# Cross-attention with a gated residual on one core: output scaling, squares and loads in another order

## The chip, the cores and the metric

The kernel runs on one core of a Trainium2 chip. The metric is the device time of one execution in microseconds (us). Engines are named as in the profile: PE is TensorE (PEld its weight loads), DVE is VectorE, ACT is ScalarE, POOL is GpSimd, SP is SyncE, whose queue issues every DMA of this kernel.

## The reference, cut to what matters

```python
def rmsnorm(v, w):
    return v * rsqrt(mean(v * v, -1) + 1e-6) * w
mem = einsum('bme,de->bmd', memory, W_mem)                # memory: 4 x 2048 x 512
scores = einsum('bnd,bmd->bnm', x, mem) / sqrt(1024)      # x: 4 x 1024 x 1024
attn = softmax(scores, -1)
context = einsum('bnm,bmd->bnd', attn, mem)
gate = sigmoid(concat([x, context], -1) @ W_gate.T + b_gate)
out = rmsnorm(x + gate * context, norm_w)                 # 4 x 1024 x 1024, fp32
```

## The kernel before

All products are fp32 in three passes: an operand is split into a high part (a cast by ACT) and a low part (a subtraction by DVE, line 305), and TensorE computes high x high, high x low and low x high into one PSUM bank. The 4096 rows of x are 32 units of 128 rows, or 16 pairs.

**Stages.** First (to about 500 us) projected queries and the x part of the gate (`zx`) are computed and stored in DRAM. Then comes the attention over the 32 units, 8 to a batch. Last comes the gate part over the 16 pairs, whose products use a seven-product scheme (Winograd's form of Strassen) with `gate_product` and `context_product`; each is 6 matmuls.

**Attention.** In step i TensorE computes the scores of unit i+1 (48 matmuls into banks 0 to 3, `scores`) and then the attention product of unit i (48 matmuls, four groups, one for each memory block). DVE takes the maxima (line 1190), ACT the exponentials (line 782). The probabilities have to be transposed over all partitions: SP stores them in DRAM and reads them back in another layout (`exchange`: stores at line 496, read back at line 502), then DVE transposes 32 x 32 blocks into PSUM (line 1219), and ACT and DVE split them. The queries of unit i+2 are loaded (line 457), cast by ACT (line 774) and their low part made by DVE (`q_split`) behind unit i+1's exponentials. TensorE waits for them (`uq_ready`) ahead of the next scores. Once per batch the memory is loaded in two layouts: `load_mt` (line 246) for the scores, `load_mn` (line 447) for the attention product, four blocks of 1 MB each. In the step that uses a new batch's first attention product (`mn_of`), some of the blocks are split ahead of the loop over groups and the others inside it; for the first unit that number is `MN_FIRST`. SP is one queue in program order: block loads, exchange, query loads and stores of results stand behind each other.

**Gate part.** TensorE's order in a pair p is gate 1, context 7 of pair p-1, gate 2, gate 3, then context 1, gate 4, context 2, gate 5, context 3, gate 6, context 4, gate 7, context 5, context 6 (`pair_c` at the end of the program). `pair_c` of DVE evacuates the gate products (`gate_part`, line 1272), multiplies gate and context (`gated`, line 1286), adds x (`residual_unit`, line 1299), transposes and splits the next pair's operands (`transpose_am`, `sums_of_am`, `split_at`) and scales a unit of an older pair (`scale`, line 1292) for its store. ACT's `pair_act` copies context products (`copy_c`, lines 860 and 869), takes sigmoids (`gate`), casts operands (`split_at`, line 796) and squares each finished unit with a sum over its row (`square`, line 875). POOL turns that sum into the root's inverse (`inverse_root`, lines 659 and 662). The result tiles `c_u` are two, one for each parity of the pair: before pair p writes `c_u[par]`, the store of pair p-2 must have landed (`out_stored`). Gate product 1 of a pair waits for all six gate evacuations of the pair before (`gz_ev`), context product 7 for context part 5.

The last pair ends with its four half units by hand: residuals (line 1495), a whole-unit square by ACT (line 935), two half squares by DVE (line 1500), a sum of the two (line 1517), POOL's two roots, `scale` of the first unit and two half scalings (line 1522).

## Time and profile before

| what | value |
|---|---|
| times of 3 runs | 1571.56, 1575.01, 1575.78 us (median 1575.01) |
| profiled execution | 1575.41 us, its span 1573.6 us |
| PE busy | 1536.4 us (98%), 6720 matmuls |
| DVE busy | 1078.2 us (69%) |
| ACT busy | 541.9 us (34%) |
| POOL busy | 36.4 us (2%) |
| DMA | 262.60 MB, mean 167 GB/s |
| granted TensorE clock, mean | 0.995 |

A time in the rows is counted from the first instruction of the span. Matmuls are pipelined and their ends are modelled, so a busy PE is not PE at its peak; the distance of starts tells its pace. A name such as `region_f` is a large SBUF region that holds many tiles; which one it is follows from the line.

### The profile page before, as it was taken

What the parts mean: (1) busy time and instruction counts of PE and PEld (TensorE: products, weight loads), DVE (VectorE), ACT (ScalarE), POOL (GpSimd) and SP (SyncE); (2) the same over time, 40 slices, a digit from 0 to 9 for tenths busy, and PEclk for the clock granted to TensorE, in tenths of its full rate; (3) what the DMA queues carried; (4) which work ended last, traced back from release to release, by engine and by line L of the source; (5) the groups of instructions that cost most, each with busy time, mean ns of one, the idle gap of its engine ahead of it and who ended that gap; (6) DMA issues with size and microseconds to landing.
All of it is one profiled execution on the core that took longest, in us unless ns stands there. A gap on an engine that the chain in (4) does not pass through costs nothing.

```text
span 1573.6 us, 21461 instructions
## 1 busy us (share of the span) xinstructions
PE 1536.4 (98%) x6720; PEld 1263.1 (80%) x6720; DVE 1078.2 (69%) x1505; ACT 541.9 (34%) x915; POOL 36.4 (2%) x70
## 2 busy tenths in 40 slices
PE   7999999999999989999999999999999999999997
PEld 5888888888888768888888878788788888788885
DVE  5654758777778754567437764577555888888887
ACT  4233342222222332244222532244222544444443
POOL 0000000000000000000000000000000001111111
PEclk9999999999999999999999999999999999999998
DMA  9998436333332866757584666747758645555553
GB/s 198 233 236 186 116 96 176 107 113 107 107 107 94 189 165 172 180 140 191 157 203 132 164 161 176 177 136 190 184 153 267 227 159 190 186 192 191 188 194 135
DMA packets 213398, 262.60 MB, mean 167 GB/s; under 512 B 19312, under 2 KB 136048, under 8 KB 213104
## 3 DMA queue, kind: packets, MB, share of 16 engines
q1 hardware_dynamic: 213360, 262.20, 59.5%
q14 instruction: 28, 0.23, 0.1%
q8 instruction: 10, 0.16, 0.0%
HBM read 170.39 MB, written 89.65 MB: 165 GB/s over the span
## 4 chain that ended last, share of the span: by engine, by line
PE 33%; DMA 13%; DVE 6%; issue 5%; SPq 3%; ACT 2%; DVEq 0%; ACTq 0%; POOL 0%; POOLq 0%
PE bank L1530 23%; PE bank L1662 10%; DMA prob_scratch<-prob 5%; DMA out<-region_f 3%; DMA region_f<-in_ctx 2%; SPq L246 2%; DMA region_f<-prob_scratch 2%; DMA am_out<-q_scratch 1%; DVE region_l L305 1%; DVE region_f L1286 1%; DVE max_part L1190 1%; DVE region_f L1292 1%; SPq L447 1%; ACT prob L782 1%; DVE region_n L305 0%
## 5 line engine op out<-in xcount | busy, mean ns | idle before, releaser
L1530 PE MATMUL bank<-region_t,region_l 128*128 128x512 f32 x1536 | 356.1, 391 | 8.4 <-DVE region_l L305 6.2
L1530 PE MATMUL bank<-region_n,region_l 128*128 128x512 f32 x1536 | 355.7, 391 | 4.1 <-DVE region_n L305 2.1
L1530 PEld LDWEIGHTS bank<-region_t,region_l 128*128 128x128 f32 x1536 | 288.9, 188 | 71.7 <-issue 11.7
L1530 PEld LDWEIGHTS bank<-region_n,region_l 128*128 128x128 f32 x1536 | 289.2, 188 | 65.7 <-issue 4.1
L1530 PE MATMUL bank<-region_t,region_n 128*128 128x512 f32 x960 | 220.4, 392 | 11.2 <-DVE region_t L305 11.2
L1530 PEld LDWEIGHTS bank<-region_t,region_n 128*128 128x128 f32 x960 | 181.7, 189 | 49.4 <-DVE region_t L305 11.6
L810 ACT CAST region_l<-bank 128x512 fp32r<-128x512 f32 x128 | 75.0, 586 | 347.2 <-DVE bank L1219 347.0
L1219 DVE STREAM_TRANSPOSE bank<-region_f 128x512 f32<-128x512 f32 x128 | 88.8, 716 | 121.7 <-DMA region_f<-prob_scratch 119.5
L305 DVE TENSOR_TENSOR region_t<-region_f,region_t 128x1024 fp32r<-128x1024 f32 (+2 forms) x77 | 110.6, 1468 | 76.4 <-ACT region_t L686 57.4
L1571 PE MATMUL bank<-region_t,region_l 128*128 128x512 f32 x576 | 135.8, 389 | 0.0
L1571 PEld LDWEIGHTS bank<-region_t,region_l 128*128 128x128 f32 x576 | 108.1, 188 | 22.4
L1662 PE MATMUL bank<-region_t,region_l 128*128 128x512 f32 x480 | 121.9, 392 | 1.8 <-DVE prob L1272 0.9
L1662 PE MATMUL bank<-region_n,region_l 128*128 128x512 f32 x480 | 120.6, 389 | 0.0
L782 ACT ACTIVATE prob<-bank,neg_max 128x512 f32<-128x512 f32 x128 | 86.2, 686 | 76.1 <-DVE neg_max L1196 72.9
L1662 PEld LDWEIGHTS bank<-region_t,region_l 128*128 128x128 f32 x480 | 89.2, 188 | 24.4 <-issue 6.4
L1662 PEld LDWEIGHTS bank<-region_n,region_l 128*128 128x128 f32 x480 | 90.0, 188 | 19.3 <-DVE region_f L1286 0.4
L737 ACT CAST region_l<-region_f 128x512 fp32r<-128x512 f32 x80 | 49.5, 623 | 158.7 <-PE bank L1571 146.5
L305 DVE TENSOR_TENSOR region_l<-region_f,region_l 128x512 fp32r<-128x512 f32 (+2 forms) x120 | 81.8, 686 | 17.8 <-ACT region_l L796 17.1
L305 DVE TENSOR_TENSOR region_l<-bank,region_l 128x512 fp32r<-128x512 f32 x128 | 86.6, 676 | 9.9 <-ACT region_l L810 9.8
L1571 PE MATMUL bank<-region_n,region_l 128*128 128x512 f32 x384 | 92.2, 389 | 0.0
L1190 DVE TENSOR_REDUCE max_part<-bank 128x1 f32<-128x512 f32 x128 | 84.4, 660 | 10.2 <-PE bank L1530 10.2
L305 DVE TENSOR_TENSOR region_n<-region_f,region_n 128x512 fp32r<-128x512 f32 (+3 forms) x70 | 78.5, 1141 | 14.6 <-ACT region_n L682 7.7
(81 smaller groups left out, 1421.9 us busy)
## 6 DMA issues: line engine op xcount, KB each, us to landing
region_f<-in_ctx SPq DMA_DIRECT2D x128, 256.0 KB, 5.4
prob_scratch<-prob SPq DMA_DIRECT2D x128, 256.0 KB, 2.7
region_f<-prob_scratch SPq DMA_DIRECT2D x128, 256.0 KB, 4.4
region_f<-in_x SPq DMA_DIRECT2D x64, 256.0 KB, 6.1
region_f<-in_x SPq DMA_DIRECT2D x128, 128.0 KB, 2.7
region_f<-in_x SPq DMA_DIRECT2D x16, 1024.0 KB, 8.1
out<-region_f SPq DMA_DIRECT2D x31, 512.0 KB, 7.1
q_scratch<-prob SPq DMA_DIRECT2D x8, 1024.0 KB, 6.3
```

Source lines behind the costliest of these rows:

```text
L246: eng.dma_start(v[SQ * q:SQ * (q + 1), :, lo:hi], src[:, chunk * q + lo:chunk * q + hi].rearrange("(b i) f -> i b f", i=SQ)).then_inc(sign ...
L305: return nc.vector.tensor_tensor(dst, src, hi.bitcast(F32), ALU.subtract)
L447: sp.dma_start(v[SQ * q:SQ * (q + 1)], mem[b, r:r + P, :].rearrange("(s i) c -> i s c", i=SQ)).then_inc(mn_loaded[j], 16)
L737: nc.scalar.copy(z_x[i][:, HI], quarter(z_f[i])).then_inc(z_hi, 1)
L782: nc.scalar.activation(prob[:, BANK * j:BANK * (j + 1)], bank[j][:], ACT.Exp, bias=neg_max[:], scale=SCALE, accum_out=sum_part[:, j:j + 1] ...
L810: nc.scalar.copy(b_pt[:, HI, TPB * g:TPB * (g + 1), :].rearrange("p k n -> p (k n)"), ps_t[g % 2][:]).then_inc(pt_hi, 1)
L1190: nc.vector.reduce_max(max_part[:, j:j + 1], bank[j][:], AX_X).then_inc(max_done, 1)
L1219: nc.vector.transpose(ps_t[g % 2][:].rearrange("p (k b i) -> p k b i", k=TPB, i=SQ), v[:, TPB * g:TPB * (g + 1)]).then_inc(pt_t, 1)
L1286: nc.vector.tensor_tensor(quad(c_u[par], u, h), src, quad(c_gate[par], u, h), ALU.mult).then_inc(gc_ev, 1)
L1530: mm = nc.tensor.matmul(dst, lhs(a), rhs(b), start=first and n == 0, stop=last and n == len(PASSES) - 1)
L1571: mm = nc.tensor.matmul(ps[:], z_x[i][:, a, t, :], z_w[i][:, b, t, :], start=opens and t == 0 and n == 0, stop=closes and t == HT - 1 and ...
L1662: mm = nc.tensor.matmul(ps[:], x[:, a, P * t:P * (t + 1)], w[n][:, b, t, :], start=opens and t == 0 and m == 0, stop=closes and t == CH - ...
```

## The change

In the attention the first unit's third memory block is loaded ahead of the first exchange and split ahead of the loop (`MN_FIRST` 3). In the four steps with `mn_of` the queries are split before the exponentials. In the two steps with `mt_ahead` DVE's four memory transposes stand behind the row sums and the query split.

In the gate part, ACT squares the pair before's units at the start of a pair, and context product 2's copy comes before product 3's. DVE scales the units of pair p-1 in pair p; before it scaled those of pair p-2. SP issues its loads and stores in a matching order. In the last pair the squares are taken by half units, three by ACT and one by DVE, POOL adds the halves, and DVE's first two residuals and the gating between them move ahead of other work.

```diff
@@ -289,7 +289,7 @@
 MTS = MB * HPJ
-MN_FIRST = 2
+MN_FIRST = 3
 MN_EARLY = 2
@@ -324,7 +324,7 @@
 U11, U22_OPEN, U12_OPEN, U22, U12, U21 = range(1, 7)
-COPY_B, COPY_12, COPY_22 = range(1, 4)
+COPY_B, COPY_22, COPY_12 = range(1, 4)
 GATE = {(0, 0): 1, (1, 1): 2, (0, 1): 3, (1, 0): 4}
@@ -514,9 +514,9 @@
 load_mn(0, 0)
-exchange(0, first=True)
 sp.wait_ge(mt_ready, HPJ * 3)
 load_mn(0, 2)
+exchange(0, first=True)
 sp.wait_ge(mt_ready, MTS)
@@ -616,29 +616,26 @@
-def pair_out(p, par, ahead=True, stored=True, am_ahead=True):
+def pair_out(p, par, ahead=True, am_ahead=True):
+    sp.wait_ge(fused_done, p * 2)
+    load_xres(p)
     if ahead:
         sp.wait_ge(gc_ev, p * NGEV)
         load_zx(p + 1, 1 - par)
-    sp.wait_ge(fused_done, p * 2)
-    load_xres(p)
-    if stored:
-        for u in range(2):
-            store_out(p - 2, par, u)
     if am_ahead:
         sp.wait_ge(ca_t, p * 2 + 4)
         load_am(p + 2)
+    for u in range(2):
+        store_out(p - 1, 1 - par, u)
 sp.wait_ge(ca_t, 4)
 load_am(2)
-pair_out(1, 1, stored=False)
+pair_out(1, 1)
 with sp.Fori(1, NPAIR // 2 - 1) as i:
...
 pair_out(NPAIR - 1, 1, ahead=False, am_ahead=False)
-for u in range(2):
-    store_out(NPAIR - 2, 0, u)
 store_out(NPAIR - 1, 1, 0)
@@ -654,8 +651,8 @@
-def inverse_root(p, u, last=0):
-    pool.wait_ge(sq_done, p * 2 + (u + 1 + last))
+def inverse_root(p, u):
+    pool.wait_ge(sq_done, p * 2 + (u + 1))
     nc.gpsimd.tensor_tensor(mean_sq[:, u:u + 1], sq_mean[:, u:u + 1], norm_eps[:], ALU.add
@@ -670,8 +667,20 @@
 pair_pool(NPAIR - 2, 0)
-inverse_root(NPAIR - 1, 0)
-inverse_root(NPAIR - 1, 1, last=2)
+def last_root(u, first, second):
+    a, b = (sum_part[:, 2 * u + h:2 * u + h + 1] for h in (u, 1 - u))
+    pool.wait_ge(sq_done, NUNIT - 2 + first)
+    nc.gpsimd.tensor_tensor(mean_sq[:, u:u + 1], a, norm_eps[:], ALU.add).then_inc(var_done, 1)
+    pool.wait_ge(sq_done, NUNIT - 2 + second)
+    pool.wait_ge(var_done, NUNIT - 2 + 2 * u + 1)
+    nc.gpsimd.tensor_tensor(mean_sq[:, u:u + 1], mean_sq[:, u:u + 1], b, ALU.add).then_inc(var_done, 1)
+    pool.wait_ge(var_done, NUNIT - 2 + 2 * u + 2)
+    nc.gpsimd.tensor_tensor(rstd[:, u:u + 1], mean_sq[:, u:u + 1], m_half[:], ALU.pow
+                            ).then_inc(rstd_done, 1)
+last_root(0, 1, 3)
+last_root(1, 2, 4)
@@ -815,9 +824,11 @@
 if softmax:
+    if mn_of is not None:
+        q_split(i + 2)
     act.wait_ge(sum_done, i + 1)
     exps(i + 1)
-    if unit_after_next:
+    if mn_of is None and unit_after_next:
         q_split(i + 2)
@@ -878,32 +889,28 @@
 seed_z(p)
+square(p - 1, 1 - par, 0, wait=i is not None)
+square(p - 1, 1 - par, 1)
 copy_c(p, 1, cb[:], ca)
-gate(p, par, 0, 0, Z11)
 if following:
     act.wait_ge(gc_prod, p * NPROD)
     act.wait_ge(ca_t, p * 2 + 4)
     split_at(1 - par, at_12, atf_12)
+gate(p, par, 0, 0, Z11)
+if i is not None:
+    act.wait_ge(out_stored[par][1], i * 16)
+copy_c(p, 2, quad(c_u[par], 1, 1), cf)
+if following:
+    act.wait_ge(ca_sum, p * 4 + 8)
+    split_at(1 - par, at_s, atf_s)
 gate(p, par, 1, 1, Z22)
...
 if following:
-    act.wait_ge(ca_sum, p * 4 + 8)
-    split_at(1 - par, at_s, atf_s)
-if i is not None:
-    act.wait_ge(out_stored[par][1], i * 16)
-copy_c(p, 2, quad(c_u[par], 1, 1), cf)
-if following:
-    gate(p, par, 0, 1, Z12)
     split_at(1 - par, at_22, atf_22)
-square(p - 1, 1 - par, 0, wait=i is not None)
-if following:
-    gate(p, par, 1, 0, Z21)
-square(p - 1, 1 - par, 1)
-if not following:
-    gate(p, par, 0, 1, Z12)
-    gate(p, par, 1, 0, Z21)
+gate(p, par, 0, 1, Z12)
+gate(p, par, 1, 0, Z21)
...
@@ -930,10 +937,12 @@
 pair_act(NPAIR - 1, 1, NPAIR // 2 - 1, following=False)
-act.wait_ge(fused_done, 2 * (NPAIR - 1) + 3)
-act.wait_ge(sq_done, NUNIT - 2)
-nc.scalar.activation(c_square, unit_tile(c_u[1], 0), ACT.Square, scale=float(D) ** -0.5,
-                     accum_out=sq_mean[:, 0:1]).then_inc(sq_done, 1)
+for n, (u, h) in enumerate(((0, 0), (1, 1), (0, 1))):
+    act.wait_ge(fused_done, 2 * (NPAIR - 1) + n + 1)
+    act.wait_ge(sq_done, NUNIT - 2 + n)
+    nc.scalar.activation(c_square[:, 0:BANK], quad(c_u[1], u, h), ACT.Square, scale=float(D) ** -0.5,
+                         accum_out=sum_part[:, 2 * u + h:2 * u + h + 1]).then_inc(sq_done, 1)
@@ -1303,37 +1312,49 @@
     gate_part(p, par, 2, zf, 1, 1)
-    if i is not None:
-        scale(p - 2, par, 0)
     gate_part(p, par, 3, za, 0, 1)
-    if i is not None:
-        scale(p - 2, par, 1)
+    if following:
+        transpose_am(p + 1, c_ain_units)
     gate_part(p, par, 4, zb, 0, 0)
     if following:
-        transpose_am(p + 1, c_ain_units)
+        sums_of_am(p + 1)
     gate_part(p, par, 5, za, 1, 1, Z22_OPEN)
     if following:
-        sums_of_am(p + 1)
         split_at(p + 1, 1, 1 - par, at_12, atf_12)
+    scale(p - 1, 1 - par, 0)
     gate_part(p, par, 6, zf, 0, 1, Z12_OPEN)
     if following:
         split_at(p + 1, 2, 1 - par, at_s, atf_s)
+    else:
+        scale(p - 1, 1 - par, 1)
     if i is not None:
         dve.wait_ge(out_stored[par][0], i * 16)
+    gated(p, par, 0, 0, cb[:], product=4)
     if not following:
-        scale(p - 1, 1 - par, 0)
-    gated(p, par, 0, 0, cb[:], product=4)
+        residual(0, 0, U11)
     gate_part(p, par, 7, za, 1, 0)
     if following:
         split_at(p + 1, 3, 1 - par, at_22, atf_22)
+        scale(p - 1, 1 - par, 1)
     context_part(p, par, 5, COPY_22, ca, 1, 1)
-    if not following:
-        scale(p - 1, 1 - par, 1)
     if following:
         context_part(p, par, 6, COPY_12, cf, 0, 1)
-        gated(p, par, 1, 1, quad(c_u[par], 1, 1), opened=U22_OPEN)
-        gated(p, par, 0, 1, quad(c_u[par], 0, 1), opened=U12_OPEN)
+    gated(p, par, 1, 1, quad(c_u[par], 1, 1), opened=U22_OPEN)
+    if not following:
+        residual(1, 1, U22 - 1)
+        context_part(p, par, 6, COPY_12, cf, 0, 1)
+    gated(p, par, 0, 1, quad(c_u[par], 0, 1), opened=U12_OPEN if following else U12_OPEN + 1)
+    if following:
         residual_unit(p, par, 0)
+LP = NPAIR - 1
+def residual(u, h, count):
+    v = quad(c_u[1], u, h)
+    dve.wait_ge(xres_loaded, NPAIR * 16)
+    dve.wait_ge(gc_ev, LP * NGEV + count)
+    nc.vector.tensor_tensor(v, v, quad(c_xres, u, h), ALU.add).then_inc(fused_done, 1)
@@ -1356,9 +1377,8 @@
     unit_max(i + 1)
-if mt_ahead is not None:
-    for h in mt_ahead[1]:
-        mt_transpose(mt_ahead[0], h)
+if mn_of is not None:
+    q_split(i + 2)
 if mt_of is not None:
@@ -1370,8 +1390,11 @@
     unit_sum(i + 1)
-    if unit_after_next:
+    if mn_of is None and unit_after_next:
         q_split(i + 2)
+if mt_ahead is not None:
+    for h in mt_ahead[1]:
+        mt_transpose(mt_ahead[0], h)
 if mt_of is not None:
@@ -1484,37 +1507,16 @@
         pair_c(i * 2 + par, par, i)
-LP = NPAIR - 1
 pair_c(LP - 1, 0, NPAIR // 2 - 1)
 pair_c(LP, 1, NPAIR // 2 - 1, following=False)
-def residual(u, h, count):
-    v = quad(c_u[1], u, h)
-    dve.wait_ge(gc_ev, LP * NGEV + count)
-    nc.vector.tensor_tensor(v, v, quad(c_xres, u, h), ALU.add).then_inc(fused_done, 1)
-def last_square(h, count):
-    v = quad(c_u[1], 1, h)
-    dve.wait_ge(fused_done, 2 * LP + count)
-    nc.vector.tensor_tensor_reduce(out=quad(c_gate[0], 1, h), in0=v, in1=v, scale=1.0 / D, scalar=0.0,
-                                   op0=ALU.mult, op1=ALU.add, accum_out=sum_part[:, h:h + 1]
-                                   ).then_inc(sq_done, 1)
-dve.wait_ge(xres_loaded, 16 * NPAIR)
-residual(0, 0, U11)
-context_part(LP, 1, 6, COPY_12, cf, 0, 1)
-gated(LP, 1, 1, 1, quad(c_u[1], 1, 1), opened=U22_OPEN)
-gated(LP, 1, 0, 1, quad(c_u[1], 0, 1), opened=U12_OPEN)
-residual(1, 1, U22)
 residual(0, 1, U12)
 gated(LP, 1, 1, 0, ca[:], product=7)
 residual(1, 0, U21)
-dve.wait_ge(sq_done, LP * 2 + 1)
-last_square(1, 2)
-last_square(0, 4)
+v = quad(c_u[1], 1, 0)
+dve.wait_ge(fused_done, 2 * LP + 4)
 dve.wait_ge(sq_done, LP * 2 + 3)
-nc.vector.reduce_sum(sq_mean[:, 1:2], sum_part[:, 0:DH], AX_X).then_inc(sq_done, 1)
+nc.vector.tensor_tensor_reduce(out=quad(c_gate[0], 1, 0), in0=v, in1=v, scale=1.0 / D, scalar=0.0,
+                               op0=ALU.mult, op1=ALU.add, accum_out=sum_part[:, 2:3]).then_inc(sq_done, 1)
 scale(LP, 1, 0)
```

## Rows read from the trace of the kernel before

**Rows 1.** Windows: busy us (count) of each engine, granted clock, DMA share, GB/s.

```profile
660.00:750.00 90.00, 90.00 (x399) 74.55 (x398) 65.15 (x94) 37.38 (x64) 0.00 (x0) 1.00 0.61 164
...
550.60:554.00 3.40, 3.40 (x9) 2.64 (x8) 1.51 (x3) 3.40 (x4) 0.00 (x0) 0.51 0.75 219
...
1308.00:1560.00 252.00, 250.44 (x1093) 203.91 (x1092) 218.12 (x320) 111.59 (x195) 31.27 (x56) 1.00 0.51 183
...
1561.70:1573.60 11.90, 0.11 (x1) 0.00 (x0) 8.52 (x16) 1.15 (x2) 3.26 (x4) 0.61 0.34 132
```

**Rows 2.** Timeline of PE, pieces with idle time before: start, us, engine, line, idle.

```profile
562.99 5.74 PE L1530 MATMUL bank<-region_n,region_l 128*128 128x512 f32 x24 [1.07 <-DVE region_l L305]
...
570.84 7.52 PE L1530 MATMUL bank<-region_n,region_l 128*128 128x512 f32 x24 [2.11 <-DVE region_n L305]
...
579.69 11.19 PE L1530 MATMUL bank<-region_t,region_l 128*128 128x512 f32 x48 [1.33 <-DVE region_l L305]
...
755.10 11.19 PE L1530 MATMUL bank<-region_t,region_l 128*128 128x512 f32 x48 [0.52 <-DVE region_l L305]
...
930.91 11.19 PE L1530 MATMUL bank<-region_t,region_l 128*128 128x512 f32 x48 [1.00 <-DVE region_l L305]
...
998.59 11.17 PE L1530 MATMUL bank<-region_t,region_l 128*128 128x512 f32 x48 [2.03 <-DVE region_l L305]
...
1108.81 11.15 PE L1530 MATMUL bank<-region_t,region_l 128*128 128x512 f32 x48 [1.13 <-DVE region_l L305]
```

**Rows 3.** Waits in the gate part: us in total, times, longest.

```profile
ACT region_f L869 <- DMA out<-region_f: 28.4, 11, 3.1
```

**Rows 4.** Timeline of all engines, one pair of the gate part.

```profile
1510.29 2.16 SPq L592 DMA_DIRECT2D out<-region_f  x2
...
1518.40 1.05 ACT L796 CAST region_t<-region_f 128x1024 fp32r<-128x1024 f32 x1
...
1522.04 1.65 PE L1662 MATMUL bank<-region_t,region_l 128*128 128x512 f32 x6
...
1522.36 0.55 POOL L662 TENSOR_TENSOR rstd<-mean_sq,minus_half 128x1 f32<-128x1 f32 x1
```

**Rows 5.** Timeline of all engines, behind the last product.

```profile
1564.77 0.69 DVE L1286 TENSOR_TENSOR region_f<-bank,region_f 128x512 f32<-128x512 f32 x1
...
1567.83 1.28 DVE L1292 SCALAR_TENSOR_TENSOR region_f<-region_f,rstd 128x1024 f32<-128x1024 f32 x1 [0.24 <-POOL rstd L662]
...
1568.03 1.49 POOL L662 TENSOR_TENSOR rstd<-mean_sq,minus_half 128x1 f32<-128x1 f32 x1
...
1569.56 1.42 DVE L1522 SCALAR_TENSOR_TENSOR region_f<-region_f,rstd 128x512 f32<-128x512 f32 x2 [0.44 <-POOL rstd L662]
```

**Rows 6.** Timeline of SP, DVE and ACT, the first unit of the attention.

```profile
542.70 1.76 SPq L447 DMA_DIRECT2D region_f<-in_ctx  x4
...
549.01 1.67 SPq L496 DMA_DIRECT2D prob_scratch<-prob  x3
...
551.58 0.34 SPq L502 DMA_DIRECT2D region_f<-prob_scratch  x1
...
560.45 1.32 DVE L1219 STREAM_TRANSPOSE bank<-region_f 128x512 f32<-128x512 f32 x2 [3.15 <-DMA region_f<-prob_scratch]
...
565.30 1.91 ACT L766 CAST region_n<-region_f 128x2048 fp32r<-128x2048 f32 x1 [2.92 <-DMA region_f<-in_ctx]
...
569.90 1.90 ACT L766 CAST region_n<-region_f 128x2048 fp32r<-128x2048 f32 x1 [2.20 <-DMA region_f<-in_ctx]
```

**Rows 7.** Timeline of SP and DVE at later steps.

```profile
638.41 1.55 SPq L496 DMA_DIRECT2D prob_scratch<-prob  x3
...
644.98 0.35 SPq L502 DMA_DIRECT2D region_f<-prob_scratch  x1
...
812.88 0.72 SPq L457 DMA_DIRECT2D am_out<-q_scratch  x1
...
1116.33 1.32 DVE L1219 STREAM_TRANSPOSE bank<-region_f 128x512 f32<-128x512 f32 x2 [6.62 <-DMA region_f<-prob_scratch]
```

More of the change, by code:

```diff
@@ L917, in _ @@
             gate(0, 0, 1, 1, Z22)
+            copy_c(0, 2, quad(c_u[0], 1, 1), cf)
             copy_c(0, 3, quad(c_u[0], 0, 1), ca)
-            copy_c(0, 2, quad(c_u[0], 1, 1), cf)
             act.wait_ge(ca_t, 4)
```

## The prediction

> **What bounds it.** I read the engines' busy shares first: TensorE is at 98%, so only time in which it waits or runs slow can be won. Its pace comes from a window without a wait: 90 us hold 397 to 399 matmuls, 0.2267 us each, so 48 of them, one unit's scores or one unit's attention product, take 10.9 us [rows 1]. All 6720 need 1523 us of a span of 1573.6; about 50 us are left, and about 10 of those are the start, before the first matmul. I then read TensorE's pieces that have idle time before them [rows 2] and looked up what each waited for.
>
> The first unit of the attention loses most: 1.1 us before its first product at 562.99, 2.1 us before 570.84 (the third memory block's low part), 1.3 us before 579.69 (the queries of the next unit) [rows 2]. After idle times of 2 us the granted clock falls to half: 9 matmuls in 3.4 us instead of 15 [rows 1], so 6 x 0.2267 = 1.4 us are lost each time. At each change of batch the queries come late: 0.5, 1.0 and 1.1 us (755.10, 930.91, 1108.81), and once more by 2.0 us at 998.59 [rows 2]. In the gate part a window of 252 us holds 1093 matmuls, worth 247.8 us: 4.2 us are lost in small pieces, though VectorE is busy for 218 and ScalarE for 112 of it, 16.5 and 8.4 us per pair of 84 matmuls (19.04 us) [rows 1]. Last, 11.9 us lie behind TensorE's last product at 1561.7 [rows 1].
>
> **Gate part.** One pair shows the stall. The output store of the pair two back is issued at 1510.29, while two loads of 1 MB are under way; ScalarE may overwrite that buffer only when it has landed, 7.6 us later, and only then casts the next operand, at 1518.40; VectorE waits for the cast, and its gate part 7 behind that lets TensorE go on at 1522.04 [rows 4]. Such waits of ScalarE sum to 28.4 us in 11 pairs [rows 3]. The change scales a pair one pair earlier. I lay VectorE's new list over TensorE's order, counted from gate product 1: the fourteen products of 1.36 us end at 1.4 (gate 1), 2.7 (context 7 of the pair before), 4.1, 5.4 (gate 2, 3), 6.8 (context 1), 8.2 (gate 4), 9.5, 10.9, 12.2, 13.6 (context 2, gate 5, context 3, gate 6), 15.0, 16.3, 17.7, 19.0 (context 4, gate 7, context 5, 6); what reads one begins 0.2 us later; half a unit takes VectorE 0.6 to 0.7 us, a whole one 1.2 to 1.3 [rows 5]. That gives: gate part 5 at 11.1 to 11.7, a split to 12.3, the scaling of unit 0 to 13.6, gate part 6 to 14.4, the wide split to 15.6, the gating to 16.2, gate part 7 at 16.5 to 17.2, a short split to 17.6, the scaling of unit 1 to 18.9, context part 5 to 19.5. The stores follow, and the buffer is wanted 9.7 us into the next pair (behind context 2): 9.7 + 19.0 - 18.9 = 9.8 us for a landing that took 7.6. So that wait goes. What is late next? VectorE's work is the same, 16.5 of 19.0 us. Gate part 7 is done at 17.2 and needed at 19.0. Context part 5, now behind a split and a scaling, is done at 19.5; product 7, which waits for it, comes at 20.4. The two squares that ScalarE now does first (1.25 us each, estimated from 1.28 for a scaling of the same tile) end near 6.6 us, and the copy behind them has its product at 6.8. The cast that held VectorE comes behind the sums, which end near 10.6, takes 1.05 us [rows 4], ends near 11.6 and is needed at 14.4. Each has 0.9 us or more to spare, so I count the whole 4.2 us. Half of it is the lower end. The reordered queue of SyncE loads xres first and the zx tile next; both had over 10 us, nothing waits for them. New waits of SyncE for the scaling hold up only the next pair's load of x, which starts 5.4 us into the pair, 5.6 us later.
>
> **Tail.** Before, gated part (1,0) ran at 1564.77, though its product ended at 1561.7 [rows 1, 5]; VectorE was still at a scaling, two residuals and two gatings. Three of these move ahead of the last product, so it can run near 1562.8: 2.0 us. One of VectorE's two last squares (0.6) goes to ScalarE, and its sum (0.15 us) goes: the last square ends 2.6 us earlier. But GpSimd has two additions per unit now and a power behind each pair. Its power took 0.55 us beside a quiet VectorE and 1.49 us (from 1568.03) beside the scaling of 1.28 us at 1567.83 [rows 4, 5]. In the new order the second unit's second addition comes behind the start of that scaling: so it ends after it, the power after that (0.25 + 0.55 + two handovers of 0.1), about 1.0 us behind the scaling's end; before it was 0.45. The first root is ready near 1565.5 (2.3 us earlier), scaling till 1566.8, the second root 1567.8, where the last scaling began at 1569.56: **1.8 us** won. If additions were not held up, 2.4.
>
> The Trainium skill (SBUF — State Buffer, section "SBUF: two separate sides") says that a VectorE operation with both inputs in SBUF locks a port pair that GpSimd's reads need, so that the loser fully blocks. By that rule the tail wins 1.8 us; without it, 2.4. The 1.49 against 0.55 us agrees with the rule.
>
> **Attention, first unit.** The third memory block's load moves ahead of the exchange of the first unit. This is the part that costs. Two blocks landed 4.6 us apart (565.30 and 569.90) [rows 6], so two of them, the first issued at 542.70, fill the queues to about 542.7 + 9.2 = 551.9. The probability stores are issued at 549.01 and the first read back at 551.58, 2.57 us later [rows 6]. Behind the second block they land at about 551.9 + 2.57 = 554.5: 2.9 us late, and everything of the exchange with them. Bounds: 0 (they pass the block) and 4.0, from a later exchange behind twelve loads, where the same step took 6.57 us (638.41 to 644.98) [rows 7]. I take 2.9. The transposition at 560.45 and the product at 562.99 go to 563.3 and 565.9. TensorE then idles 4.0 us and runs slow for a slice behind it (1.4 us). In exchange the third block's casts are done before (three casts of 1.9 us [rows 6] and three low parts little longer fit between the exponentials, near 551, and 563.3), the fourth lands near 568, its casts end near 573.5, and TensorE needs it after 36 matmuls and the slow slice, at 575.5: both other stalls and the other slow slice go. The queries, cast ahead of the exponentials, are there by 570. Scores of the next unit begin at 565.9 + 10.9 + 1.4 = 578.2 instead of 579.69: **1.5 us**. Without the delay, 574.0: 5.7 us. With 4.0 us of delay, 0.4 us.
>
> **Attention, queries at the batch changes.** They stop being late there (0.5, 1.0 and 1.1 us). But what TensorE wins against the exchange it may lose again. At the first two the next wait is the query load, issued behind twelve block loads at 812.88 [rows 7] and its like before 998.59; those come behind the exchange in SyncE's queue, and the exchange doesn't move. I count 0 there. At the third no such wait follows; the next transposition starts at 1116.33, and by the 2.54 us between 560.45 and 562.99 the product can start at 1118.9, where it started at 1108.81 + 11.0 = 1119.8 [rows 2, 6, 7]: **0.9 us**. The transpositions moved behind the queries (four of 1.2 us) end 2 us before the next exchange lands: 0.
>
> **Sum.** 4.2 + 1.8 + 1.5 + 0.9 = 8.4 us off the profiled execution's 1575.41, which is 0.4 above the median 1575.01: 1567.0.
>
> **Rivals.** A: the stores pass the block load. Against: 6.57 us behind loads [rows 7]. For: that queue was longer, with small pieces. It gives 4.2 us more: **1562.8**, chance 0.2. The Trainium skill (DMA: Bandwidth & Descriptors, section "Queues, rings and completion order") says that an engine takes a ring's descriptors in order; by it A can't be. B: the gate part keeps half its stalls because VectorE, 87% busy, is late after its two scalings: 4.2 / 2 less, **1569.1**, chance 0.15; for it speaks that 0.9 us of room is small. C: the batch-change wins stay (0.5 + 1.0 more): **1565.5**, chance 0.15. D, slower: the stores, now issued at the pair's end, run into the loads of the next pair and take long. The point is 9.8 us, and as the cast has 2.8 us more room, 12.6 in all. At 13.5 us each pair stalls 0.9 us, 14 x 0.9 = 12.6, which takes the place of the 4.2 lost now: 1567.0 + 12.6 = **1579.6**, chance 0.03. Against: 7.6 us with both loads in flight [rows 4]. E: the change does nothing in the attention, 2.4 us less won: 1569.4, 0.07. My forecast has 0.4.
>
> **Numbers.** A measurement can tell about 0.3%, 4.7 us, so the mark is 1570.3. The range reaches from A, with a bit for C beside it, to B and E with the runs' spread: 1562 to 1571. Faster 0.87, within 0.3% 0.1, slower 0.03.
>
> **What would show it.** The wait of ScalarE's context copies for the output stores gone [rows 3], and no idle TensorE piece in the gate part from the third pair. One idle piece of about 4 us before the first unit's product, then half clock, and none before the third block. Idle of 1 us or so where the first two batches' gains are given back, and a later q wait grown by as much. The last scaling begins 8 us earlier than 1569.56. Wrong if the first exchange isn't late, if SyncE's stores take over 10 us, or if context part 5 holds product 7.

## The result and the profile after

The changed kernel takes **1569.90 us** (median of 20 runs, 1567.14 to 1571.97). The kernel before takes 1572.92 us in the same series (20 runs, 1569.89 to 1575.88), so two of the three runs known ahead of the prediction (1575.01 and 1575.78; median of the three 1575.01) lay at the slow end of its own spread. The ratio is 0.998, interval 0.9973 to 0.9987: 3.0 us faster. A second series gave 0.9979 (0.997 to 0.9987). That is real, but less than the 0.3% set as the mark, and 2.9 us short of the forecast 1567.0.

The profiled execution took 1568.30 us, span 1566.5 (before: 1575.41 and 1573.6). To see where 7.1 us of span went I take the start of the n-th matmul on TensorE, which is the same work in every kernel here, and add up by stretch. "First unit" is the 96 matmuls from the scores of unit 1 (n = 2352) to the scores of unit 2 (n = 2448); "gate part" runs from the first full pair (n = 5478) to the last product (n = 6719), "tail" from that product's start to the end of the span.

| stretch, us | before | after | after, again |
|---|---|---|---|
| start to n = 2352 | 549.13 | 549.28 | 548.59 |
| first unit | 30.56 | 31.62 | 29.69 |
| rest of attention to n = 5478 | 695.60 | 693.59 | 696.61 |
| gate part | 286.13 | 281.43 | 281.43 |
| tail | 12.17 | 10.55 | 10.56 |

**Gate part.** Windows of the kernel after (us, then busy time and count of PE, PEld, DVE, ACT, POOL; granted clock; DMA share; GB/s), for a stretch of the gate part, the tail, and the half-clock stretch of the first unit:

```profile
1300.00:1552.00 252.00, 252.00 (x1113) 208.67 (x1112) 224.03 (x324) 117.70 (x196) 25.30 (x52) 1.00 0.49 186
1556.20:1566.50 10.30, 0.11 (x1) 0.00 (x0) 6.32 (x10) 1.12 (x4) 3.39 (x5) 0.67 0.26 102
...
566.40:573.20 6.80, 6.20 (x15) 4.85 (x16) 6.46 (x10) 3.50 (x5) 0.00 (x0) 0.50 0.23 48
```

252 us now hold 1113 matmuls where they held 1093 [rows 1]: TensorE is at its pace of 0.2267 us throughout. ScalarE's waits in the gate part say why. In the kernel after:

```profile
ACT bank L871 <- PE bank L1664: 38.1, 14, 2.7
ACT region_f L876 <- DVE region_f L1281: 36.0, 30, 2.6
ACT prob L876 <- DVE prob L1281: 30.3, 28, 2.1
ACT region_n L886 <- DVE region_f L1308: 29.2, 29, 1.3
```

Every wait is for something that is computed; the row that waited for the output stores [rows 3] has no successor. In one pair the stores are issued behind the loads, and the second waits in SyncE's queue for its scaling (timeline of the kernel after):

```profile
1503.00 0.41 SPq L612 DMA_DIRECT2D region_f<-in_x  x1
...
1503.66 0.41 SPq L586 DMA_DIRECT2D prob<-zx_scratch  x1
...
1505.57 0.40 SPq L582 DMA_DIRECT2D region_f<-am_scratch  x1
...
1511.36 5.59 SPq L592 DMA_DIRECT2D out<-region_f  x2
```

By then the loads of x and zx have landed. The page gives the median landing of all 31 stores, in the kernel after and in the kernel before:

```profile
out<-region_f SPq DMA_DIRECT2D x31, 512.0 KB, 2.6
...
out<-region_f SPq DMA_DIRECT2D x31, 512.0 KB, 7.1
```

**First unit.** TensorE's timeline of the kernel after:

```profile
549.28 12.77 PE L1532 MATMUL bank<-region_t,region_l 128*128 128x512 f32 x48 [2.07 <-ACT prob L791]
567.00 14.06 PE L1532 MATMUL bank<-region_n,region_l 128*128 128x512 f32 x48 [4.95 <-DVE region_l L305]
580.90 11.04 PE L1532 MATMUL bank<-region_t,region_l 128*128 128x512 f32 x48
...
767.07 3.23 PE L1532 MATMUL bank<-region_n,region_l 128*128 128x512 f32 x13 [0.62 <-DVE region_l L305]
...
822.88 7.33 PE L1532 MATMUL bank<-region_t,region_l 128*128 128x512 f32 x31 [1.13 <-DVE region_l L305]
```

One idle piece of 5.0 us, then all 48 products in one piece, and no wait for the queries at 580.90: the three waits of before [rows 2] are one. But the clock was at half (1.2 GHz) for 6.8 us from the end of that idle piece on, not for 3.4. The last two rows are the first batch change: TensorE starts its scores without a wait (755.41) and waits at the product behind them, and again at the next query load.

SyncE's timeline of the kernel after shows the price of the early load, 5.86 us from the stores to the first read back instead of 2.57 [rows 6]:

```profile
542.85 3.71 SPq L447 DMA_DIRECT2D region_f<-in_ctx  x8
549.16 1.67 SPq L496 DMA_DIRECT2D prob_scratch<-prob  x3
555.02 0.34 SPq L502 DMA_DIRECT2D region_f<-prob_scratch  x1
```

**Tail.** All engines, timeline of the kernel after, answering to [rows 5]:

```profile
1559.49 1.01 POOL L679 TENSOR_TENSOR rstd<-mean_sq,minus_half 128x1 f32<-128x1 f32 x1
...
1560.47 0.18 POOL L674 TENSOR_TENSOR mean_sq<-sum_part,norm_eps 128x1 f32<-128x1 f32 x1
1560.53 1.28 DVE L1301 SCALAR_TENSOR_TENSOR region_f<-region_f,rstd 128x1024 f32<-128x1024 f32 x1 [0.43 <-POOL rstd L679]
1560.80 1.06 POOL L677 TENSOR_TENSOR mean_sq<-mean_sq,sum_part 128x1 f32<-128x1 f32 x1
1561.84 0.33 SPq L592 DMA_DIRECT2D out<-region_f  x1
1561.94 0.55 POOL L679 TENSOR_TENSOR rstd<-mean_sq,minus_half 128x1 f32<-128x1 f32 x1
1562.52 1.42 DVE L1524 SCALAR_TENSOR_TENSOR region_f<-region_f,rstd 128x512 f32<-128x512 f32 x2 [0.71 <-POOL rstd L679]
```

GpSimd's second addition for unit 1 starts beside VectorE's scaling and ends with it, 1.06 us; the same kind of addition takes 0.18 us a moment earlier. The root is ready 0.7 us behind the scaling.

### The profile page after: what moved, and what is told of

Its sections match the earlier page's. It is cut to its first block, busy times and chain, and to the rows that moved or that the text cites. A ratio compares the mean times of both kernels' runs of the same rounds, so it can differ in the third digit from the quotient of the medians.

```text
span 1566.5 us, 21464 instructions
## 1 busy us (share of the span) xinstructions
PE 1532.7 (98%) x6720; PEld 1264.5 (81%) x6720; DVE 1080.2 (69%) x1502; ACT 549.2 (35%) x919; POOL 33.3 (2%) x72
## 4 chain that ended last, share of the span: by engine, by line
PE 77%; DMA 11%; SPq 4%; DVE 4%; issue 3%; ACT 1%; POOL 0%; ACTq 0%; DVEq 0%; POOLq 0%
PE bank L1532 39%; PE bank L1573 19%; PE bank L1664 19%; DMA prob_scratch<-prob 5%; SPq L246 2%; DMA region_f<-prob_scratch 2%; DMA region_f<-in_ctx 2%; DMA am_out<-q_scratch 1%; DVE region_l L305 1%; DVE max_part L1199 1%; DMA region_f<-in_L_xattn_W_gate 1%; SPq L447 1%; DVE bank L1228 0%; DVE region_n L305 0%; SPq L337 0%
## 5 line engine op out<-in xcount | busy, mean ns | idle before, releaser
L1532 PEld LDWEIGHTS bank<-region_n,region_l 128*128 128x128 f32 x1536 | 290.0, 189 | 70.0 <-DVE region_l L305 5.4
L1532 PEld LDWEIGHTS bank<-region_t,region_n 128*128 128x128 f32 x960 | 181.1, 189 | 50.2 <-DVE region_t L305 12.5
L1664 PEld LDWEIGHTS bank<-region_n,region_l 128*128 128x128 f32 x480 | 90.0, 188 | 19.1 <-DVE region_f L1295 0.4
L1199 DVE TENSOR_REDUCE max_part<-bank 128x1 f32<-128x512 f32 x128 | 84.5, 661 | 12.3 <-PE bank L1532 12.3
L1573 PEld LDWEIGHTS bank<-region_n,region_l 128*128 128x128 f32 x384 | 72.1, 188 | 15.0
```

What stands on the lines that cost most here:

```text
L1199: nc.vector.reduce_max(max_part[:, j:j + 1], bank[j][:], AX_X).then_inc(max_done, 1)
L1532: mm = nc.tensor.matmul(dst, lhs(a), rhs(b), start=first and n == 0, stop=last and n == len(PASSES) - 1)
L1573: mm = nc.tensor.matmul(ps[:], z_x[i][:, a, t, :], z_w[i][:, b, t, :], start=opens and t == 0 and n == 0, stop=closes and t == HT - 1 and ...
L1664: mm = nc.tensor.matmul(ps[:], x[:, a, P * t:P * (t + 1)], w[n][:, b, t, :], start=opens and t == 0 and m == 0, stop=closes and t == CH - ...
```

## The experiments

Twelve kernels ran, each with one profile. The first four shared 35 runs of the kernel before (median 1571.68), the next four 20 (1572.89), the last four 27 (1571.86); ratios are to those.

**1. Load back, the rest changed.**

```
-        MN_FIRST = 3
+        MN_FIRST = 2
...
             load_mn(0, 0)
+            exchange(0, first=True)
             sp.wait_ge(mt_ready, HPJ * 3)
             load_mn(0, 2)
-            exchange(0, first=True)
```

> The changed kernel with its early load taken back: the third block is again loaded behind the first exchange and split inside the loop; the query order, the gate part and the tail stay changed. Theory 1 (the early load delays the first exchange by 4 us and costs more than it gives): the changed kernel lost 1.2 us up to the scores of the third unit against before; without the load the queries ahead of the exponentials should give 1.5 us there instead, so this kernel is 2.5 to 3 us faster than the changed one, about 6 us under the kernel before (ratio 0.996). Theory 2 (the load is a gain or nothing, and the small total comes from elsewhere: the gate part's gain is smaller in most executions than in the profiled one): this kernel is as fast as the changed one or slower, ratio 0.998 or more.

Measured 1569.36 us (12 runs), ratio 0.9984 (0.9974 to 0.9993): the same as the changed kernel, so theory 1 (2.5 to 3 us faster than that) is out. Stores to read back is 2.58 us again, and two stalls are back in other places: 2.8 us inside the first product and 0.7 us ahead of the second unit's. First unit 30.54 us.

**2. The load alone.** The kernel before, with the same five lines of experiment 1 the other way round.

> The kernel before with the early load alone (third block ahead of the first exchange, three blocks split ahead of the loop). Theory 1: one idle piece of 5 us before the first unit's product, two slices at half clock, and in all 1 to 1.5 us slower than before. Theory 2: both later stalls of the first unit go at no price, 4 us faster.

1571.36 us (12 runs), ratio 0.9995 (0.9985 to 1.0004); stores to read back 5.70 us, first unit 30.71. It is neither slower by 1 us nor faster by 4, as the two theories had it. With experiment 1: the early load is worth nothing either way. What it takes away and what it costs are equal within the noise.

**3. Gate part and tail alone.** The new orders of both; load, queries and transpositions as before (in step_act and step_dve):

```
-                    if mn_of is not None:
-                        q_split(i + 2)
                     act.wait_ge(sum_done, i + 1)
                     exps(i + 1)
-                    if mn_of is None and unit_after_next:
+                    if unit_after_next:
                         q_split(i + 2)
...
```

> The kernel before with the gate part's new order and the tail by halves alone (no early load, queries and transposes as before). Both theories put the gain here; by the two profiles the gate part gives 4.7 us and the tail 1.6: 6.3 us under before, ratio 0.996. Theory 2 wants it at 3 us. The difference to the run without the early load is what the query order gives by itself: 1.5 us at the first unit and some tenths at the third batch change by theory 1.

1569.00 us (11 runs), ratio 0.9985 (0.9977 to 0.9994): 2.7 us, as theory 2 had it, and not the 6.3 us of the two profiles. The whole gain of the change is here.

**4. The load sooner.** As changed, but the third block is loaded ahead of SyncE's wait for the zx stores, so that nothing stands behind it but one more block:

```
+            sp.wait_ge(mt_ready, HPJ * 3)
+            load_mn(0, 2)
             for i in range(3):
                 sp.wait_ge(zx_stored[i], 16 * NPAIR)
             load_mn(0, 0)
-            sp.wait_ge(mt_ready, HPJ * 3)
-            load_mn(0, 2)
             exchange(0, first=True)
```

> The changed kernel with the third block's load issued ahead of SyncE's wait for the last zx stores, so about 3 us sooner and ahead of the first block's load in the queue. Theory 1: the queue is empty sooner, the first exchange is 2 us instead of 4 us late, the idle piece before the first unit's product is 3.3 instead of 5.3 us, one slice at half clock instead of two: 2 to 3.4 us faster than the changed kernel. A rival (the delay doesn't come from the queue but from splits of three blocks on ScalarE and VectorE, or from reading back into the same memory): the idle piece stays 5 us and the time that of the changed kernel.

1566.48 us (12 runs), ratio 0.9964 (0.9955 to 0.9974). Stores to read back: 4.65 us. The idle piece ahead of the product was expected at 3.3 us with 3.4 us of half clock behind it; this profile has 6.0 us and 6.8 us, no better than with the load in the changed kernel's place (4.4 to 6.5 us in five profiles). The runs are faster all the same, by 2.9 us against experiment 1 in the same series.

**5. The scaling held.**

```
-            scale(LP, 1, 0)
             dve.wait_ge(rstd_done, NUNIT)
+            scale(LP, 1, 0)
```

> The changed kernel, with VectorE's scaling of the last pair's unit 0 held until GpSimd has the root of unit 1 too. Theory 1 (GpSimd is blocked while VectorE runs an operation with two SBUF inputs): GpSimd's second addition for unit 1, which took 1.06 us beside that scaling, takes 0.2 to 0.3 us again, its power 0.55 us; the root of unit 1 is there about 0.8 us sooner, and the three last scalings run one behind the other: last product to end of span 11.0 us instead of 10.56 (+0.5). Rival (that addition takes about 1 us by itself, for instance because it follows right on another): it still takes 1.06 us, the root comes as late as now, the tail is 11.8 us (+1.3).

GpSimd's timeline of this kernel:

```profile
1563.35 0.18 POOL L674 TENSOR_TENSOR mean_sq<-sum_part,norm_eps 128x1 f32<-128x1 f32 x1
1563.68 0.19 POOL L677 TENSOR_TENSOR mean_sq<-mean_sq,sum_part 128x1 f32<-128x1 f32 x1
1563.95 0.55 POOL L679 TENSOR_TENSOR rstd<-mean_sq,minus_half 128x1 f32<-128x1 f32 x1
```

The addition takes 0.19 us, and the root ends 5.70 us behind the last product's start instead of 6.57, 0.87 us sooner. That settles it for theory 1: GpSimd's operation was blocked by the scaling, it was not slow by itself.

All 14 profiles together show which operations of VectorE block it. Of GpSimd's additions, 263 began while VectorE ran an operation with two inputs in SBUF (residuals, gatings with a copied product, low parts, squares, scalings); every one of them ended 0.04 to 0.05 us behind the end of that operation, and took up to 1.16 us. Another 158 began beside a transpose or beside an operation that reads one input from PSUM; they took 0.19 us, as beside a quiet VectorE. The Trainium skill (SBUF — State Buffer, section "SBUF: two separate sides") has the rule: a VectorE operation with two SBUF inputs and a GpSimd operation that reads SBUF use one port pair in turns, each for its whole instruction. This run and these counts agree with it. The tail, though, is 11.49 us, not 11.0: the scalings end 0.32 us later, and the last stores are now issued 0.7 us behind unit 0's whole store instead of 1.5 and land in 2.6 us instead of 2.0. Its time, 1568.34 us (7 runs, 0.997, 0.9959 to 0.9981), can't show half a microsecond.

**6. Stores ahead of the loads.** The kernel before with one edit in pair_out; scaling, squares and ScalarE's order stay:

```
+                if stored:
+                    for u in range(2):
+                        store_out(p - 2, par, u)
                 if ahead:
                     sp.wait_ge(gc_ev, p * NGEV)
                     load_zx(p + 1, 1 - par)
                 sp.wait_ge(fused_done, p * 2)
                 load_xres(p)
-                if stored:
-                    for u in range(2):
-                        store_out(p - 2, par, u)
```

> The kernel before, whose only edit is in SyncE's queue of the gate part: the two output stores of a pair are issued ahead of the two 1 MB loads of zx and x instead of behind them; the scaling stays where it was, two pairs late. Theory 1 (what stalled the gate part was only the landing of those stores behind loads): stores land in 2.6 to 3.5 us instead of 7, ScalarE's waits for them (28.4 us in 11 pairs before) fall under 5 us, the gate part from gate product 1 to the last product takes 281.4 to 282 us instead of 283.5 to 286.1, the tail stays 12.2 us, and the time is 2 us under the kernel before. Rival A (stores share the engines with whatever is in flight, wherever they stand in the queue): landing stays near 7 us and the gate part at 283.5 or more. Rival B (the loads, now behind the scaling's wait, come late): a new wait for zx or x, gate part over 284 us.

1570.10 us (11 runs), ratio 0.9982 (0.9973 to 0.9991). SyncE's timeline of this kernel, the same pair as [rows 4]:

```profile
1505.51 2.16 SPq L592 DMA_DIRECT2D out<-region_f  x2
1507.92 0.41 SPq L586 DMA_DIRECT2D prob<-zx_scratch  x1
1508.51 0.51 SPq L612 DMA_DIRECT2D region_f<-in_x  x1
```

The pair runs 4.5 us earlier here (what was won till then), so the stores are issued at the same point of it, within 0.3 us; only the loads stand behind them now. From the page, the stores' landing:

```profile
out<-region_f SPq DMA_DIRECT2D x31, 512.0 KB, 2.7
```

No wait of ScalarE for them is left, the gate part takes 281.43 us to the hundredth as in the changed kernel, and the tail is 12.08. Theory 1 holds without remainder: not the lateness of the scaling but the two loads ahead of the stores made the stall. The whole reordering of the gate part is matched by moving three lines of a queue.

**7. Sooner, attention otherwise old.** Experiment 4 with the queries and transpositions put back as in experiment 3.

> As e4_load_sooner (third memory block loaded ahead of the wait for the zx stores), but with the queries behind the exponentials and the transpositions behind the row maxima again, as in the kernel before. It tells whether the early load needs the queries ahead. Theory 1 (what e4 gained over the changed kernel, 3.4 us, is the load's place alone; queries ahead are given back): 1566 to 1567.5 us, the same as e4. Rival (with the load in its place the queries are what is late next, 1.2 us at the third unit and 0.5 to 1.0 at each change of batch): 1568 us or more.

1566.67 us (5 runs), ratio 0.9959 (0.9946 to 0.9972), as experiment 4. The queries ahead add nothing.

**8. Squares whole.** The changed kernel with the last pair's squares of before:

```
-            for n, (u, h) in enumerate(((0, 0), (1, 1), (0, 1))):
-                act.wait_ge(fused_done, 2 * (NPAIR - 1) + n + 1)
...
+            act.wait_ge(fused_done, 2 * (NPAIR - 1) + 3)
+            act.wait_ge(sq_done, NUNIT - 2)
+            nc.scalar.activation(c_square, unit_tile(c_u[1], 0), ACT.Square, scale=float(D) ** -0.5,
...
+            last_square(1, 2)
+            last_square(0, 4)
```

> The changed kernel, with the squares of the last pair as in the kernel before: ScalarE squares unit 0 whole, VectorE both halves of unit 1 behind it and adds them, GpSimd has one addition per unit. The order of the gatings and residuals stays the new one. Theory 1 (GpSimd blocked beside two-input operations of VectorE): the second root comes 0.75 us later at its start, but with one addition less to be blocked; the last scalings start 0.3 us later, tail 10.9 us instead of 10.56; so of the tail's 1.6 us the halves are 0.3 and the order 1.3. Rival (halves are worth what they take off VectorE, 0.6 + 0.15 us): tail 11.3 us or more.

Tail 10.71 us, 0.16 more than with halves: 0.3 was expected, the rival's 0.75 is out. So of the tail's 1.6 us the new order gives 1.5 and "the tail by halves" almost nothing, because VectorE's saved time is spent waiting for a root that is blocked beside the scaling, as these rows of its timeline show:

```profile
1559.67 1.28 DVE L1289 SCALAR_TENSOR_TENSOR region_f<-region_f,rstd 128x1024 f32<-128x1024 f32 x1
1559.84 1.16 POOL L656 TENSOR_TENSOR mean_sq<-sq_mean,norm_eps 128x1 f32<-128x1 f32 x1 [0.48 <-DVE sq_mean L1515]
```

Its time is 1567.54 us (7 runs, 0.9969, 0.9958 to 0.998).

**9 to 12. One more series,** with the changed kernel itself, the sooner load alone on the kernel before, and experiments 3 and 7 again.

> The changed kernel itself once more, so that it stands in one series with the three kernels beside it (the kernel before moved by 1.2 us between two series). Theory 1 (its own gain is 2.5 to 3 us, and the early load behind the zx stores is worth nothing): 2 to 4 us under the kernel before of this series, the same as e11_gate_tail_again within 1.5 us. Rival (the first unit costs it 1 us or more against the old order, as in its one profile, +1.1): e11_gate_tail_again is 1 us or more faster than this.

> The kernel before, and of the change only the third memory block's load, put ahead of the wait for the zx stores. Theory 1 (the place of the load was worth 3 us in e4_load_sooner and is independent of the gate part): 2.5 to 3.5 us under the kernel before, with no TensorE idle time from the queries or the third block at 570 to 580. Rival (what e4 showed was mostly its series and the gate part): within 1 us of the kernel before, as e2_load_alone was; index of the first scores behind the first product (2448) not more than 1 us sooner than before.

> e3_gate_tail_alone again in one series with the others (kernel before with the new order of the gate part and the tail, attention as before). Theory 1: 2.5 to 4 us under the kernel before: the gate part at 281.4 us and the tail at 10.56 us, as in every kernel with these orders. Against e12_best_again it stands for the early load's worth in its best place: by theory 1 it is 2.5 us slower than that, by the rival (that gain was chance) within 1 us.

> e7_sooner_rest_old again, in one series with the changed kernel: gate part and tail new, third memory block loaded ahead of the wait for the zx stores, queries and transpositions as before. Theory 1: 1565.5 to 1567.5 us, 5.5 to 6.5 us under the kernel before and 2 us or more under the changed kernel. Rival (run to run spread made it look better in its series): within 1 us of e11_gate_tail_again and of the changed kernel.

| kernel | median us (runs) | ratio, interval |
|---|---|---|
| changed | 1568.71 (11) | 0.9979, 0.997 to 0.9987 |
| sooner alone | 1570.05 (11) | 0.9988, 0.9979 to 0.9997 |
| gate and tail | 1568.92 (8) | 0.9974, 0.9963 to 0.9985 |
| gate, tail, sooner | 1565.97 (7) | 0.9964, 0.9952 to 0.9977 |

Gate and tail alone equals the whole change again. Sooner alone wins 1.8 us, less than the 2.5 expected, and with gate and tail 5.9 us. That version beats the kernel before in both its series (0.9959 and 0.9964). Against the changed kernel it is 2.7 us faster in the one series that has both, by 7 runs against 11; experiments 5 and 8, the changed kernel but for its tail, were 1.7 and 0.9 us slower than it in the other, the second within the noise. TensorE's timeline of "sooner alone", with idle time of 2.5 us where the changed kernel had 5.0 (the shortest of its kind: the other three profiles with the load there have 3.9, 4.0 and 6.0):

```profile
549.37 12.77 PE L1530 MATMUL bank<-region_t,region_l 128*128 128x512 f32 x48 [2.07 <-ACT prob L782]
564.64 12.57 PE L1530 MATMUL bank<-region_n,region_l 128*128 128x512 f32 x48 [2.50 <-DVE region_l L305]
577.05 8.32 PE L1530 MATMUL bank<-region_t,region_l 128*128 128x512 f32 x36
```

**The first unit over all 14 profiles** (mean and range of each group, us). To product: from n = 2352 to the first product.

| load of the third block | profiles | stores to read back | to product | its 48 products | both |
|---|---|---|---|---|---|
| behind the exchange | 5 | 2.6 | 14.3 | 16.4 | 30.7 (30.2 to 31.2) |
| ahead of it, behind zx stores | 5 | 5.8 | 17.6 | 13.2 | 30.8 (29.7 to 31.6) |
| ahead of the zx stores' wait | 4 | 4.5 | 16.1 | 13.0 | 29.1 (27.7 to 30.6) |

The profiles give the sooner load 1.7 us in this stretch; the timed runs give it 1.8 us by itself and about 3 us with the gate part and the tail. Where the rest of it lies isn't shown.

## Why the prediction was right or wrong

The time lay in the range and on the side said. That is partly luck: the sum was 8.4 us and the gain is 3.0, but the sum was taken off the profiled execution's 1575.41, 2.5 us above the median that 20 runs gave; 8.4 - 3.0 - 2.5 = 2.9 us is the error. The time also lies next to rivals with chances of 0.15 (B, 1569.1) and 0.07 (E, nothing from the attention, 1569.4). E's mechanism is what the runs show in the attention; B's is not what they show in the gate part. Term by term:

**Gate part, 4.2 us.** Mechanism right, and shown twice: by the change itself, and by experiment 6 with the landing alone. The list of VectorE's work held: all 11 profiles in which the stores no longer stand behind the loads have 281.42 to 281.47 us, the pace of TensorE, so rival B (half the stalls stay) and D (stores slow in the next pair's loads; they landed in 2.6) are out. Against the profile of before it won even 4.7. The step that failed is "I count the whole 4.2 us", read as a property of the kernel: the term was too large by 1.1 us. It was one execution's: three profiles with the old gate part lost 4.7, 2.1 and 2.4 us against 281.43, with landings of 6.9 to 7.1 us. The stall hangs on when each landing ends, and the one profile at hand was the worst of three. Their mean, 3.1 us, agrees with what experiment 6 won (2.8). "Half of it is the lower end" was nearer to the truth than the value taken.

**Tail, 1.8 us.** Measured 1.6, in every profile (12.08 to 12.24 before, 10.55 to 10.57 after). The blocked addition came as worked out, and experiment 5 shows it to be the cause. The last scaling began 7.0 us earlier than 1569.56, 8 were said. Two parts were off against each other: the first root came 1.8 us sooner behind the last product's start, not 2.3, and the second was ready 0.7 us behind the scaling's end, not 1.0. VectorE's square and sum that go were put at 0.6 and 0.15 us of the way; experiment 8 finds 0.16 for all that the halves do.

**Attention, first unit, 1.5 us.** The sign of every step was right: the exchange came late by 3.3 us (2.9 said, from the times when two blocks land; rival A, stores pass the loads, would have shown 2.57 us to the read back; it is this measurement that rules it out), and all later waits fell together into one. What failed is the second half: "Scores of the next unit begin at 565.9 + 10.9 + 1.4". The 48 products took 13.2 us on the mean, not 12.3, since behind the one long idle time the clock was at half for 6.8 us in 6 of 9 profiles with the load early in either place, against never more than 3.4 us at a time with the load old. The 48 products took 12.5 us on the mean in the three profiles with 3.4 us of it and 13.4 in the six with 6.8. The slow slice itself was priced low, too: 1.4 us by a count of nine matmuls, where the two pieces of 24 matmuls in [rows 2] differ by 7.52 - 5.74 = 1.8 us. With 0.4 us for the exchange, 0.9 for the products, and 0.3 because the 48 products take 16.4 us on the mean of the old profiles and 16.7 in the one of before, the 1.5 us are gone: measured 0.1 slower.

**Attention, queries, 0.9 us at the third change.** Wrong. The expected win and its counterpart can be laid side by side as the distance from the last matmul ahead of the scores to the scores, plus the distance from there to the next product. Third change: 1.52 + 10.99 = 12.51 us before, 0.23 + 12.00 = 12.23 after; over eight profiles with the queries behind 12.5 on the mean, over six with them ahead 12.6. The step was "the next transposition starts at 1116.33": it started 11.7 to 12.0 us behind the start of the exponentials in the old order, but 12.0 to 13.4 us behind in the new one, so the product had nothing to gain. Why the exchange lands later there isn't settled; the read back is issued at the same distance from the stores (2.4 to 2.5 us), and its fourth piece lands 8.2 to 8.6 us later in the old order and 8.5 to 10.0 in the new one, so it is in the landing. In two of the six profiles the wait grew to 2.2 us and more and cost a half-clock stretch besides. That the first two changes are given back was right (rival C is out): at the first change with 0.6 us of idle time at the next product and 1.1 us at the query load behind it. A wait at that load, 0.8 to 1.3 us, stands in all six profiles with the queries ahead and in four of the eight without. From n = 2448 to 5478 the mean is 695.3 us with queries ahead and 695.1 without.

Together by profiles: 3.1 + 1.6 - 0.1 - 0.2 = 4.4 us. The timed runs say 3.0 and 3.2, with intervals reaching to 4.2 and 4.7; I can't tell whether 1 us more is lost in executions that weren't profiled.

## What to carry to other kernels

When a buffer waits for its store, look first at what stands ahead of the store in its queue: three lines moved there did all that a new order of three engines did for the gate part. A transfer moved to an earlier place was paid here by the exchange issued behind it; give it a place where nothing urgent follows closely, and expect several small waits to become one large one that also costs clock. Short GpSimd operations that others wait for are blocked while VectorE reads two inputs from SBUF; yet holding VectorE back for them cost more than it gave here (experiment 5: the root 0.87 us sooner, the tail 0.9 us longer). And where a stall depends on when a transfer lands, profile the kernel twice before you price it: one execution showed 4.7 us for something worth 3.

## What the runs showed of the hardware that was not expected

The same 512 KB stores, issued at the same point of a pair, landed in 7.1 us behind two 1 MB loads and in 2.7 us ahead of them, and the loads behind them held up nothing. One block (1 MB) more ahead of the exchange moved its stores' landing by 3.2 us in five of five profiles (5.70 to 5.86 against 2.57 to 2.60), and by 1.9 us where the two blocks were issued 8.0 us ahead of those stores instead of 6.3. A GpSimd addition that began beside a VectorE operation with two SBUF inputs ended 0.04 to 0.05 us behind it, 263 times in 263. In the tail the last 256 KB stores landed in 2.0 us when unit 0's store had a start of 1.5 us, and in 2.6 us when it had 0.7 (experiment 5 alone).
